# Second cross attention of a decoder on one core: keys as such, regrouped by transfers, and four heads' scores in one pass

## The reference, cut to what matters

```python
q = (x @ Wq + bq)         # 8 x 56 x 128, as 16 heads of 8
k = (ctx @ Wk + bk)       # 8 x 1500 x 128, Wk is 64 x 128
v = (ctx @ Wv + bv)
a = softmax(q @ k.T / sqrt(8))     # per batch and head: 56 x 1500
x = x + (a @ v) @ Wo + bo
```

## Time and profile before

| | us |
|---|---|
| median of 3 runs (lowest, highest) | 669.24 (666.65, 669.37) |
| profiled execution: its time | 664.66 |
| profiled execution: its span | 662.9 |
| busy: PE, DVE, ACT, POOL | 621.5, 493.9, 353.0, 379.3 |
| granted TensorE clock, mean | 1.00 |

### The profile page before, as it was taken

One profiled execution on the slowest core, in us unless ns is written; L12 is line 12 of the kernel. 1 busy time (PEld: TensorE's weight loads), 2 busy tenths in 40 slices (PEclk: granted clock), 3 DMA queues, 4 the chain that ended last, 5 costly groups with the idle time before them and its releaser, 6 DMA issues.

```text
span 662.9 us, 19804 instructions
## 1 busy us (share of the span) xinstructions
PE 621.5 (94%) x8743; PEld 464.5 (70%) x8743; DVE 493.9 (75%) x796; ACT 353.0 (53%) x550; POOL 379.3 (57%) x272
## 2 busy tenths in 40 slices
PE   8889898899999999999898979999999999999997
PEld 4566785677777777777776556677777777777774
DVE  3666738799989889896665764877888988977543
ACT  2065663655646646647354316286586586664443
POOL 1362453388888888574220326078988988955400
PEclk9999999999999999999999999999999999999999
DMA  9600003000000002000032000001101100000000
GB/s 267 244 1 3 3 2 134 2 2 3 2 2 2 2 2 95 4 2 2 1 132 120 1 0 1 1 2 48 48 2 49 48 2 2 2 2 2 2 1 15
DMA packets 4657, 20.87 MB, mean 31 GB/s; under 512 B 500, under 2 KB 756, under 8 KB 4572
## 3 DMA queue, kind: packets, MB, share of 16 engines
q1 hardware_dynamic: 4572, 19.60, 8.8%
HBM read 19.37 MB, written 0.23 MB: 30 GB/s over the span
## 4 chain that ended last, share of the span: by engine, by line
PE 72%; DVE 12%; ACT 8%; issue 5%; POOL 2%; DMA 1%; POOLq 0%; DVEq 0%
PE psum L1125 18%; PE psum L1024 10%; PE psum L1066 5%; PE psum L1073 5%; PE psum L212 5%; PE psum L1068 5%; DVE scratch L1241 3%; PE psum L1003 3%; PE psum L1030 1%; PE psum L241 1%; PE psum L1042 1%; POOL scratch L626 1%; ACT scratch L1159 1%; ACT lv L286 1%; PE psum L1036 1%
## 5 line engine op out<-in xcount | busy, mean ns | idle before, releaser
L1226 POOL TENSOR_TENSOR scratch<-scratch 125x896 bf16<-125x896 f32 x136 | 238.5, 1765 | 117.7 <-ACT scratch L1206 117.5
L1206 ACT ACTIVATE scratch<-psum 125x896 f32<-125x896 f32 x192 | 173.1, 915 | 147.0 <-PE psum L1125 145.8
L1241 DVE TENSOR_REDUCE scratch<-psum 128x1 f32<-128x500 f32 x336 | 209.8, 671 | 14.1 <-PE psum L1024 6.4
L1125 PE MATMUL psum<-scratch 128*125 128x448 bf16 (+2 forms) x624 | 143.6, 355 | 0.5 <-ACT scratch L1206 0.2
L1066 PE MATMUL psum<-tok,scratch 125*128 125x65 bf16 x1344 | 108.9, 195 | 1.8 <-DVE kT L1286 1.8
L1068 PE MATMUL psum<-tok,scratch 125*128 125x64 bf16 x1344 | 108.3, 192 | 0.0
L1066 PEld LDWEIGHTS psum<-tok,scratch 125*128 125x128 bf16 x1344 | 95.3, 97 | 15.6 <-issue 2.6
L1024 PE MATMUL psum<-scratch 128*128 128x500 bf16 x273 | 102.3, 375 | 3.3 <-DVE scratch L1241 2.0
L1068 PEld LDWEIGHTS psum<-tok,scratch 125*128 125x128 bf16 x1344 | 90.2, 99 | 16.1
L1125 PEld LDWEIGHTS psum<-scratch 128*125 128x125 bf16 (+2 forms) x624 | 80.0, 136 | 26.1 <-ACT scratch L1206 0.8
L1226 DVE TENSOR_TENSOR scratch<-scratch 125x896 bf16<-125x896 f32 x56 | 68.6, 1227 | 18.1 <-ACT scratch L1206 17.0
(11 more groups left out here) (337 smaller groups left out, 896.7 us busy)
## 6 DMA issues: line engine op xcount, KB each, us to landing
nrm<-turned_dram SPq DMA_DIRECT2D x8, 750.0 KB, 4.6
raw<-ctx_dram SPq DMA_DIRECT2D x4, 672.0 KB
w_third<-fifth_dram SPq DMA_DIRECT2D x3, 636.0 KB, 5.4
w_third<-third_dram SPq DMA_DIRECT2D x2, 844.0 KB, 21.1
w_third<-third_dram SPq DMA_DIRECT2D x2, 843.5 KB, 19.2
w_fourth<-fourth_dram SPq DMA_DIRECT2D x3, 542.5 KB, 5.7
w_first<-first_dram SPq DMA_DIRECT2D x1, 996.0 KB, 4.8
w_second<-second_dram SPq DMA_DIRECT2D x1, 834.0 KB, 6.7
```

The source lines that it names most:

```text
L1125: mm = nc.tensor.matmul(bank(S + f, HALF, CP), lhs[0:rows, CP * c:CP * c + CP], rhs[0:rows, HALF * f:HALF * f + HALF], start=(rows == 128) ...
L1206: nc.scalar.activation(CR["p"][0:CP, n % RING, :].rearrange("p (f n) -> p f n", f=2), psum[0:CP, S:S + 2, 0:HALF], ACT.Exp).then_inc(self. ...
L1226: ops.tensor_tensor(CR["pl"][0:CP, n % RING, :], CR["p"][0:CP, n % RING, :], p_high(n % RING), ALU.subtract).then_inc(done, 1)
L1241: nc.vector.tensor_reduce(mxp[:, r, t:t + 1], bank(B, TB), X_AXIS, ALU.max).then_inc(self.aux_freed, 1)
```

## The change

Keys are made for all heads at once: one float32 matmul of `x_wk` (64 x 128) against 500 columns of transposed context (unit K, three a batch), whose result, with the bias added, is split into `key_high` (ScalarE) and `key_low` (VectorE), 128 rows of 16 heads x 8. SyncE then regroups them by transfers within the core's memory: for each of four groups of four heads, the 32 rows of high, low and high again go under each other into `key_group`, 12 transfers of 32 x 500 bf16 for each 500 columns, beside a row of ones on row 96. There are two slots, for even and odd batches, and one `key_high` and `key_low`, which is written again when the transfers out of it have landed.

Queries are projected once with the packed `x_wq` (128 x 128) and scaled by a mask per head position, so that each of four copies keeps one head of every group. Unit Q is then four float32 matmuls with `spread`, a selection of 32 rows three times over. The result is block-diagonal: for a group of four heads, 224 columns of 97 rows (high, high, low, shift). The scores of a chunk are four matmuls of 224 columns, one for each group, in a single pass. The maxima are 24 matmuls of 112 query columns by 500 (8 tiles x 3 blocks), over 64 rows. One more low part of every batch goes to GpSimd (chunk 1). `keyed_placement` is the hand-written order: K of batch b + 2 in chunks 0 and 9 of batch b, Q in chunk 1 (before chunk 2), M from chunk 2 (before chunk 4).

For batches 0 and 1 the six K units stand in the last six chunks of `cross1`, on banks 0, 1 and 7; `cross1` waits for all six low parts before its last two chunks' sums. Context copies (`context_act`, `context_low`) and the memsets of ones and zeros for `cross2` are gone. `cross1` is otherwise unchanged.

```diff
-        turned = [flat[:, CTX * i:CTX * i + CTX] for i in range(TURNED)]
+        turned = params["first"][0:64, 0:CTX]
+        def key_group(slot, g):
+            at = 4 * CTX // 2 * slot + CTX // 2 * g
+            return flat[:, at:at + CTX // 2].bitcast(BF16)
...
+            if keyed:
+                return n % 2 == 0 if n >= CHUNKS * (BATCH - 1) + 3 else n % CHUNKS not in (0, 11)
...
+        def keyed_placement(front, outputs, keys):
+            at = [[] for _ in range(CHUNKS)]
+            maxima = iter(KEYED[2:2 + MAXIMA * TBLK])
+            def some(c, n):
+                at[c] += [[u] for u in itertools.islice(maxima, n)]
+            if keys:
+                at[0] += [[("K", 0)], [("K", 1)]]
+            if front:
+                at[1] += [KEYED[0:2]]
+                some(2, 3)
+                some(3, 1)
+            if outputs:
+                at[3] += [[]] * (not front) + [[("N", 0)], [("N", 1)]]
+            if front:
+                some(3, 1)
+                for c in range(4, 11):
+                    some(c, 3 if c < 9 else 2)
+                at[11] += [[], [KEYED[-2]], [KEYED[-1]]]
+            if outputs:
+                at[5] += [[("O", 0)]]
+            if keys:
+                at[9] += [[("K", 2)]]
+            return at
...
+                        for g in range(GROUPS):
+                            mm = nc.tensor.matmul(psum[0:96, self.home(idx + g // 2), 224 * (g % 2):224 * (g % 2) + 224],
+                                                  par("spread", 96 * g, 96 * g + 96), qT[:, :, 56 * b:56 * b + 56],
+                                                  start=True, stop=True)
+                            if g % 2:
+                                mm.then_inc(self.aux_ready, 1)
+                        return
...
+                elif kind == "M" and self.keyed:
+                    t, r = k // MAXIMA, k % MAXIMA
+                    if k == 0 and b:
+                        pe.wait_ge(self.q_high, 2 * b)
+                    elif k == 0:
+                        pe.wait_ge(self.front_act, 1)
+                        pe.wait_ge(self.front_dve, 1)
+                    if r == 0:
+                        pe.wait_ge(keys_loaded[i][t], 192 * (b // 2 + 1))
+                    mm = nc.tensor.matmul(bank(B, TB, QROWS), CR["qa", i][0:64, QROWS * r:QROWS * r + QROWS],
+                                          key_group(i, r // 2)[0:64, TB * t:TB * t + TB], start=True, stop=True)
...
+            def keys_pe(self, pe, b, t, B):
+                if b == 0:
+                    pe.wait_ge(loaded["keys"], 16)
+                pe.wait_ge(turned_loaded[t], 16 * (b + 1))
+                return nc.tensor.matmul(bank(B, TB), par("x_wk", rows=64), turned[:, TB * t:TB * t + TB],
+                                        start=True, stop=True)
+            def keys_act(self, act, b, t, B):
+                cols = slice(TB * t, TB * t + TB)
+                if b:
+                    act.wait_ge(keys_loaded[(b - 1) % 2][t], 192 * ((b - 1) // 2 + 1))
+                nc.scalar.activation(key_high[:, cols], bank(B, TB), ACT.Identity, bias=col("x_bk")
+                                     ).then_inc(keys_high, 1)
+            def keys_dve(self, dve, b, t, B):
+                cols = slice(TB * t, TB * t + TB)
+                dve.wait_ge(keys_high, TBLK * b + t + 1)
+                nc.vector.scalar_tensor_tensor(key_low[:, cols], bank(B, TB), col("x_bk"), key_high[:, cols], ALU.add,
+                                               ALU.subtract).then_inc(keys_low, 1)
...
+                            pe.wait_ge(ones_loaded, 32)
+                        for g in range(GROUPS):
+                            mm = nc.tensor.matmul(psum[0:CP, S + g // 2, 224 * (g % 2):224 * (g % 2) + 224],
+                                                  key_group(i, g)[0:97, CP * c:CP * c + CP],
+                                                  CR["qa", i][0:97, 224 * g:224 * g + 224], start=True, stop=True)
...
+                    if self is cross1 and b == BATCH - 1 and c >= 6:
+                        kb, t = (c - 6) // TBLK, (c - 6) % TBLK
+                        if kb:
+                            pe.wait_ge(keys_low, t + 1)
+                        else:
+                            self.wait_freed(pe, self.index("O", 0, BATCH - 2))
+                        cross2.keys_pe(pe, kb, t, SIDE[t]).then_inc(keys_made, 1)
+                if self is cross1:
+                    pe.wait_ge(keys_low, 2 * TBLK)
...
-                    if self is cross1 and b == BATCH - 1 and c in (2, 4, 6, 8):
-                        cross2.context_act(act, (c - 2) // 4, (c - 2) // 2 % 2)
-                    if self is cross2 and b < BATCH - 2 and c in (4, 6):
-                        self.context_act(act, b + 2, c // 2 - 2)
+                    if self is cross1 and b == BATCH - 1 and c >= 6:
+                        act.wait_ge(keys_made, c - 5)
+                        cross2.keys_act(act, (c - 6) // TBLK, (c - 6) % TBLK, SIDE[(c - 6) % TBLK])
...
-                    if self is cross1 and b == BATCH - 1 and c in (3, 5, 7, 9):
-                        cross2.context_low(dve, nc.vector, (c - 3) // 4, (c - 3) // 2 % 2)
+                    if self is cross1 and b == BATCH - 1 and c >= 6:
+                        cross2.keys_dve(dve, (c - 6) // TBLK, (c - 6) % TBLK, SIDE[(c - 6) % TBLK])
...
-                    if self is cross2 and b < BATCH - 2 and c in (5, 8):
-                        self.context_low(pool, nc.gpsimd, b + 2, c // 3 - 1)
...
+        def keyed_lead_pe(pe, ready):
+            pe.wait_ge(loaded["fifth"], 16 * PIECES)
+            pe.wait_ge(*ready[0])
+            for k in range(2):
+                nc.tensor.matmul(bank(2 + k, width(LEAD[0])), par("x_wq"), x2[:, LEAD[0]], start=True, stop=True
+                                 ).then_inc(*q3.done(f"qa{k}"))
...
+            def keys_in(b, t):
+                cols = slice(TB * t, TB * t + TB)
+                for g in range(GROUPS):
+                    rows = slice(32 * g, 32 * g + 32)
+                    for k, part in enumerate((key_high, key_low, key_high)):
+                        sp.dma_start(key_group(b % 2, g)[32 * k:32 * k + 32, cols], part[rows, cols]
+                                     ).then_inc(keys_loaded[b % 2][t], 16)
...
+            for b in range(2):
+                for t in range(TBLK):
+                    sp.wait_ge(keys_low, TBLK * b + t + 1)
+                    turned_in(b + 1, t)
+                    keys_in(b, t)
...
+            for b in range(2, BATCH):
+                for t in range(TBLK):
+                    if t != 1:
+                        for lot in (0, 1) if t == 0 else (2,):
+                            sp.wait_ge(keys_low, TBLK * b + lot + 1)
+                            if b < BATCH - 1:
+                                turned_in(b + 1, lot)
+                    sp.wait_ge(cross2.scores, CHUNKS * (b - 2) + 4 * t + 4)
+                    keys_in(b, t)
...
+    c["head_scale"] = ((P[:, None] // 8 % 4 == np.arange(4)[None, :]) * 8.0 ** -0.5).astype(f)
+    m = np.zeros((128, 4, 3, 32), f)
+    for p in range(128):
+        m[p, p // 32, :, p % 32] = 1
+    c["spread"] = m.reshape(128, 384)
```

More of the change, by code:

```diff
@@ L26 @@
 TOKENS = 4
-TURNED = 2
+GROUPS, MAXIMA, QROWS = 4, 8, 112
 PIECES = 4
@@ L59, in sig @@
             return Signal(sem(name), products)
-        params = {p: sb("w_" + p, list(a.shape)) for p, a in packs.items() if p not in ("fifth", "turned")}
+        params = {p: sb("w_" + p, list(a.shape)) for p, a in packs.items() if p not in ("fifth", "turned", "keys", "ones_row")}
+        params["keys"] = params["first"][:, CTX:CTX + packs["keys"].shape[1]]
         params["fifth"] = params["third"][:, 0:packs["fifth"].shape[1]]
@@ L153, in build @@
             CR["yb", i] = R.take([CTX], BF16)
-        for n, at in (("ya", CTX * TURNED), ("yb", CTX * TURNED + CTX // 2)):
-            CR[n, 2] = flat[:, at:at + CTX // 2].bitcast(BF16)
+        key_high, key_low = CR["ya", 0], CR["yb", 0]
         held = R.at
@@ L930, in __init__ @@
                         "front_act", "front_dve", "front_low"))
-                self.turns = 0 if biased else 2
-                self.front = FRONT[2 - self.turns:]
+                self.turns = 0 if keyed else 2
+                self.front = KEYED if keyed else FRONT
                 self.order = [(u, 0) for u in self.front]
@@ L937, in __init__ @@
                     self.steps.append([])
-                    for lots in placement(b < BATCH - 1, b > 0, self.turns):
+                    placed = (keyed_placement(b < BATCH - 1, b > 0, b < BATCH - 2) if keyed
+                              else placement(b < BATCH - 1, b > 0))
+                    for lots in placed:
                         self.steps[-1].append([])
@@ L950, in freed @@
             def freed(self, idx):
-                return sum(u[0] not in "TN" and (u[0], b) != ("Q", 0) for u, b in self.order[:idx + 1])
```

(23 more changed lines are left out.)

284 lines of the change are left out of this document (141 added, 143 removed).

## The result

| kernel | median, us | lowest to highest | span of the profiled execution | granted clock |
|---|---|---|---|---|
| before | 668.83 (4 runs) | 666.65 to 669.37 | 662.9 | 1.000 |
| changed | 727.70 (4 runs) | 727.08 to 729.91 | 725.3 | 0.978 |

The changed kernel is slower: ratio 1.0893, 95% interval 1.0858 to 1.0927, 59 us. Between the two profiled executions it is 62.4, since the one of the kernel before, with the clock at 1.000 throughout, was 4 us faster than its median. The forecast was 673 with a range to 681, a change of +5.1. Its direction was right and its size was far off, so the question is where the 57 us between 5.1 and 62.4 come from.

What follows compares the result with a forecast made beforehand. TensorE was taken as the bound, VectorE having only 3.7 us to spare in a middle batch. Run -9.0, front +1.2, tail +11.4 and clock +1.5 gave +5.1 us: forecast 673 us, range 662 to 681.

Steps and rivals of the forecast that it cites:

- TensorE in a middle batch: Batches 1 to 5 of the second attention: shorter scores against added maxima and keys, net minus 1.0, TensorE needing 24.3 us.
- Period 25.3: Middle batches: VectorE works without a gap from the first maximum, period 25.3 instead of 25.46, five batches giving -0.8 us.
- b = 0, b = 6, b = 7: First and last two batches of the second attention: fewer tasks make them shorter by 2.4, 2.4 and 3.4 us.
- Front: Stretch 405 to 428 before the batches: 24 instead of 21 maxima at 0.60 us, net +1.2 (bounds 0 and +2.5).
- Tail: First attention's last six chunks: batch 1's key copies wait for batch 0's transfers, issued 0.42 us apart, delaying sums by +11.4.
- Rival 1: First attention's end: SyncE issues the short transfers quickly, tail +3.7 instead of +11.4, about 664 us; chance 0.22.
- Clock: Behind TensorE's 4.7 us idle in the first attention's end: a lower clock slows sums and projection, +1.5 (bounds 0 and 4).
- The transfers of later batches: Middle batches: SyncE's 39 transfers take 16 us of 25 to issue and land in time, priced at nothing.
- Rival 2: Score matmuls: halved, they no longer cover the slow weight load, +6 to +9 in all, 680 us; chance 0.07.
- Rival 3: Middle batches: VectorE's waits vanish, period 24.3, -5 over five batches, net about 0, 668 us; chance 0.20.
- Rival 4: Second attention: nothing saved, period stays 25.46 everywhere but in b = 7, net +10 to +12, 679 us; chance 0.06.

Runs made afterwards that it cites:

- e2_rows96: Changed kernel with the maxima contracting over 96 rows instead of 64, the first one waiting for the queries' low half: 702.7 us.
- e9_stages: e8_fixed with a second buffer for batch 1's keys, so that their copies need not wait for batch 0's transfers: 675.5 us.
- e11_front: Changed kernel without the filler matmuls between the maxima of the first batch's front: 726.4 us.
- e8_fixed: Changed kernel with 96-row maxima (a batch's first two 64), 128-wide weights, e6_whole's regrouping, third key lot behind the last maximum: 684.3 us.
- e12_later: e9_stages with the first maximum of a batch half a chunk's sums later: 678.9 us against 668.3 for the kernel before, ratio 1.019.
- e6_whole: Changed kernel with the keys of batches 0 and 1 regrouped once per batch, 12 transfers of 3000 bytes a row instead of 36 of 1000: 720.7 us.

## Why the prediction was wrong, step by step

- **TensorE in a middle batch, forecast 24.3: the step that failed.** It priced a maximum over 64 rows at the 0.21 of one over 128, and scores and sums as if nothing stood between them. Measured 30.67. (Its own terms, 25.42 less 1.0, give 24.4.) Of the 6.4 too little, the changes between 64 and more rows explain 5.4 (e2_rows96), and the keys 3 x (1.03 - 0.87) = 0.5. The Trainium skill ("TensorEngine Tiling (Array Packing)", section "Key Properties") says that changing the tiling mode drains TensorE. It names no price, and it does not say there that an ordinary matmul over 64 rows changes the mode. The traces agree with such a drain: about 0.11 us each way in both kernels, and nothing at 96 rows; that a drain is the cause is not shown. This rule spoke against the change, as did the 0.90 in the trace of the kernel before, and neither was weighed.
- **Period 25.3, bound by VectorE.** Wrong in the changed kernel: 31.06, bound by TensorE. In e9_stages, where only two maxima of a batch and the keys are over 64 rows, most of the argument holds: from the first maximum on, VectorE works through 15.8 us (forecast 16.7 with the third lot of keys in it). The first maximum comes 10.4 after the small reduce (forecast 8.65); the third lot moved there (1.05) and two dearer lots (0.3) are most of that. Total 26.1. That VectorE alone sets it is not shown: SyncE's queue is as full.
- **b = 0, b = 6, b = 7 (-2.4, -2.4, -3.4).** The same step failed here. The first full period was to be 21.8 and is 29.57; the period with no keys was to be 23.0 and is 27.73. They stay under a middle batch, by 1.5 and 3.3 (forecast 3.5 and 2.3). The stretch behind the last small reduce gained 0.9.
- **Front, +1.2.** It took three more maxima at VectorE's pace of 0.60. From the first maximum to the last it was 13.05 before and is 18.59, 5.5 more. The pace was TensorE's 0.78, and what is new in it is once more the change of rows: with the same fillers and 96 rows it is 0.54 to 0.59 (e9_stages). e11_front, without the fillers, gains 3.3, which the clock then asks back in part. Some 1.7 more was lost between the projection's start and the first maximum, 0.6 of it in the projection (3.31 against 2.74).
- **Tail, +11.4 (bounds 8.0 to 14.4).** The mechanism was right in every step: copies on ScalarE wait for transfers of batch 0, sums behind them, projection late. The pitch was mis-sized: 0.42 from transfers out of DRAM, where the regrouping reads inside the core. The 39th issue starts 23.3 behind the first (314.61 to 337.94), 0.61 apart, where 16.0 was forecast: 7.3 of the 9.8 too little. The forecast let the landing begin with the last issue's start. Issue and landing took 2.5 instead of 1.7: 0.8. The sums at the lower clock are 1.0, and the first lot was 0.5 late. Rival 1, a quick issue, was wrong. The 50 ns that the prediction takes from the Trainium skill ("DMA: Bandwidth & Descriptors", section "Anatomy of one DMA") stand there for transfers issued from GpSimd; they say nothing of SyncE's queue.
- **Clock, +1.5 (0 to 4).** It fell, as forecast, and the size was right: 1.0 in the sums ahead of the projection and 0.8 behind them.
- **The transfers of later batches, at nothing.** Right in the changed kernel, where no matmul of a middle batch waits for one, but only because its period is 31 us. The 39 issues of a batch were priced at 16 us and take 26.3. In e8_fixed, e9_stages and e12_later, at periods near 26, the cover is gone, as the prediction said it might be: key copies on ScalarE wait up to 3.0, 2.5 and 3.6 us for a landing.
- **Rivals 2, 3, 4.** Rival 2 fell with e2_rows96. Rival 3 needed VectorE's waits gone; its 668 was never reached. Rival 4's period of 25.46 was too short as well.

The budget, by spans: 34.8 us more in the run, of which six middle periods at 5.4 for row changes give 32; 21.4 in the tail, of which a second buffer takes 14.5 away (e9_stages; the first buffers' whole regrouping included); 7 in the front, 5.5 of it between the maxima. With the three cured, e9_stages' span is still 10.8 above before: 8.8 up to the small reduce of b = 0 (6.9 of it the tail), 2.8 in the run (a fall of the clock is 2.3 of that), and 0.8 given back at the end. By the times on one chip it is 7.2 above (675.5 against 668.3). What the single pass of scores saves, the keys' float32 matmuls take.

## What to carry to other kernels

Count how often TensorE goes between contractions over 64 rows and longer ones. If short ones stand singly among long ones, fill them up, here to 96 rows, or put them together (e11_front's front; elsewhere not tried). Take the price of an issue from a transfer with the same source and destination, and ask how many issues stand between a buffer's last reader and its next writer. Fewer issues brought the projection forward by 6.3 us (e6_whole), the second buffer by another 7.1 (e9_stages against e8_fixed). When an engine is freed in one place, look at the pieces of the chain one by one before saying who binds next.

## Not expected of the hardware

- Going between 64-row and longer contractions costs TensorE about 0.11 us each way; a matmul over 96 rows is 0.11 to 0.13 us cheaper there than one over 64. Lengths under 64 were not tried. Scores whose passes contract over 128 and 65 rows (the first attention of the kernel before) take 0.76 to 0.79 for four, the same as over 128 and 97, so 65 rows cost nothing.
- Rows are not the only thing that does it: behind unit A of the kernel before, with 128 rows and weights of one column, seven sums take 0.32 instead of 0.21. No run looks into that.
- SyncE issues a transfer out of the core's own memory every 0.59 to 0.63 us, for 32 and 128 rows and for 1000 and 3000 bytes a row, and one out of DRAM every 0.42 at 1000 bytes a row, but every 0.60 with 64 rows of 2000 bytes. Crossing from rows 32 to 63 to rows 0 to 31 costs nothing (0.590 against 0.592).
- The granted clock fell behind some single short waits of TensorE. In e9_stages the first maxima of four batches waited 0.36 to 1.09 us. Behind that of 1.09 the stretch 520 to 525 was at 0.70, and that period took 28.4; behind another of 0.99 the period took 26.7 without a fall. So a fall costs some 2 us, and what decides over it stays open.
